# The last pair of expert half tiles: placed by one-hot products and added by GpSimd, or scattered with the rest

## The reference, cut to what matters

```python
def _L1_ffn_ref(hidden_states, gate_w, gate_up_proj, down_proj):
    B, S, H, E, I, TOPK = (1, 256, 512, 16, 256, 2)
    ...
    p = jax.nn.sigmoid(logits)
    p = p / jnp.sum(p, axis=-1, keepdims=True)
    w, idx = jax.lax.top_k(p, TOPK)
    w = w / jnp.sum(w, axis=-1, keepdims=True)
    combine = jnp.sum(jax.nn.one_hot(idx, e, dtype=w.dtype) * w[..., None], axis=1)
    gu = jnp.einsum('th,ehf->etf', x, gate_up_proj)
    gate, up = jnp.split(gu, 2, axis=-1)
    inter = jax.nn.silu(gate) * up
    y = jnp.einsum('eti,eih->eth', inter, down_proj)
    out = jnp.einsum('eth,te->th', y, combine.astype(y.dtype))
```

## Time and profile before

| what | value |
|---|---|
| median of 3 runs | 2191.06 us (2190.95 to 2192.75) |
| the profiled execution | 2190.56 us |
| its span, first to last instruction | 2188.8 us |
| PE busy | 2079.7 us, 95% of the span |
| DVE, ACT, POOL busy | 1566.5, 1253.0, 573.9 us |
| data moved | 202.02 MB |

### The profile page before, as it was taken

One profiled execution on the slowest core, in us unless ns is written; L12 is line 12 of the kernel. 1 busy time (PEld: TensorE's weight loads), 2 busy tenths in 40 slices (PEclk: granted clock), 3 DMA queues, 4 the chain that ended last, 5 costly groups with the idle time before them and its releaser, 6 DMA issues. The chain is left out here.

```text
span 2188.8 us, 36050 instructions
## 1 busy us (share of the span) xinstructions
PE 2079.7 (95%) x11652; PEld 1792.7 (82%) x11652; DVE 1566.5 (72%) x3714; ACT 1253.0 (57%) x3253; POOL 573.9 (26%) x1480
## 2 busy tenths in 40 slices
PE   7999999999999999999899999999999999599992
PEld 6888988988888778887788888888888887388882
DVE  6777687677779884434677777777777777777775
ACT  5554455445455533324776766677676666567771
POOL 2001011001001002223333434433343433145541
PEclk9999999999999999999999999999999999799996
DMA  7232122122220220002111211111111111278886
GB/s 255 78 116 74 66 87 90 59 90 68 85 78 34 75 75 1 1 0 78 49 59 49 72 53 57 48 57 48 57 64 71 48 40 39 87 272 291 292 272 257
DMA packets 78500, 202.02 MB, mean 92 GB/s; under 512 B 8688, under 2 KB 38408, under 8 KB 66208
## 3 DMA queue, kind: packets, MB, share of 16 engines
q1 hardware_dynamic: 68672, 179.37, 23.5%
q0 software_dynamic: 7520, 16.80, 2.3%
q10 hardware_dynamic: 2176, 4.19, 0.5%
HBM read 179.09 MB, written 29.10 MB: 95 GB/s over the span
## 5 line engine op out<-in xcount | busy, mean ns | idle before, releaser
L1255 DVE TENSOR_TENSOR l_pT_lo<-bank,l_pT_hi 128x512 fp32r<-128x512 f32 x256 | 175.3, 685 | 69.7 <-ACT l_pT_hi L1081 69.7
L742 PE MATMUL bank<-l_wkv_hi,l_ctxT 128*128 128x512 f32 (+1 forms) x768 | 222.3, 361 | 2.7 <-DVE l_v_lo L1255 1.6
L1075 ACT ACTIVATE l_probs<-l_scored,l_nbias 128x256 f32<-128x256 f32 x256 | 128.5, 505 | 165.7 <-DVE l_nbias L1328 165.7
L742 PE MATMUL bank<-l_wo_hi,l_oT_hi 128*128 128x512 f32 x512 | 209.1, 408 | 0.7 <-DVE l_oT_lo L1255 0.7
L742 PE MATMUL bank<-xnT_hi,l_wq_hi 128*128 128x512 f32 x512 | 209.0, 408 | 0.8 <-DVEq L1561 0.7
L742 PE MATMUL bank<-l_wo_hi,l_oT_lo 128*128 128x512 f32 x512 | 200.5, 392 | 0.0
L742 PE MATMUL bank<-xnT_hi,l_wq_lo 128*128 128x512 f32 x512 | 200.2, 391 | 0.0
L742 PE MATMUL bank<-l_wo_lo,l_oT_hi 128*128 128x512 f32 x512 | 199.9, 390 | 0.0
L742 PE MATMUL bank<-xnT_lo,l_wq_hi 128*128 128x512 f32 x512 | 199.8, 390 | 0.0
L1081 ACT CAST l_pT_hi<-bank 128x512 fp32r<-128x512 f32 x256 | 150.8, 589 | 67.5 <-PE bank L841 67.4
L1343 DVE TENSOR_SCALAR l_probs<-l_probs,l_rden 128x256 f32<-128x256 f32 x512 | 181.3, 396 | 9.0
(11 more groups left out here) (307 smaller groups left out, 5754.0 us busy)
## 6 DMA issues: line engine op xcount, KB each, us to landing
l_ctxT<-ctx_split SPq DMA_DIRECT2D x63, 1024.0 KB, 4.8
moe_raw_gu<-in_L_ffn_gate_up_proj SPq DMA_DIRECT2D x31, 1024.0 KB, 6.7
moe_raw_dn<-in_L_ffn_down_proj SPq DMA_DIRECT2D x31, 512.0 KB, 5.5
l_raw_a<-in_L_xattn_Wq SPq DMA_DIRECT2D x16, 512.0 KB, 5.9
l_raw_a<-in_L_xattn_Wo SPq DMA_DIRECT2D x16, 512.0 KB, 5.8
x_sb<-in_x SPq DMA_DIRECT2D x4, 1024.0 KB, 8.8
l_v_next<-l_kn SPq DMA_DIRECT2D x16, 256.0 KB, 2.0
l_v_lo<-l_v_next SPq DMA_DIRECT2D x16, 256.0 KB, 2.7
```

The lines of the kernel that those rows point to most:

```text
L742: mm = nc.tensor.matmul(out, a[x], b[y], start=(i == 0), stop=(i == n - 1))
L1075: ins = nc.scalar.activation(probs[u % 2][:, t, :], src, ACT.Exp, bias=nbias[:, i:i + 1], scale=scale, accum_out=rsum[:, i:i + 1])
L1255: nc.vector.tensor_tensor(pair[1], src, pair[0].bitcast(F32), ALU.subtract).then_inc(done, 1)
```

## The change

The 45 halves 0 to 44 are scattered as before. The last pair, halves 45 and 46, is not. `SENT = HALVES - 2` counts those that are sent.

- Where no scatter writes, `y_rows` must hold zeros: the FFN stage fills all 8.39 MB with zeros in four transfers from one tile.
- The routing marks which tokens stand in the last pair. GpSimd counts the numbers 0 to 2047 in one instruction and casts them in four. DVE works out each token's weight for the last pair (`weigh_last`, round 3) and two one-hot matrices of 128 rows by 2048 tokens, one for each half (`mark_tokens`, rounds 6 and 9).
- Behind the last down products, the results of halves 45 and 46 are split into high and low parts. For each of the 16 token tiles TensorE multiplies them by the one-hot matrices (4 products of 512 columns), ScalarE scales the sum by the weight, and GpSimd adds it to `x_sb`. DVE's two additions for a tile wait for that.
- The loads of `y_rows` wait for 15 scatters in each of three semaphores instead of for 16, 16 and 15. The buffers `w_gu[1]` are taken before `w_gu[0]`.
- In round 46, `down(44)` and its copy come ahead of `gate_up_products(46)` and of `gate(46)`.
- For lack of semaphores those of the FFN stage are cleared and used again; the clearing stands ahead of the two gain loads of the second attention.

```diff
@@ attention_stage, sync
             if rms:
+                for s in k.past_sems:
+                    sp.sem_clear(s)
@@ ffn_stage
+        zeros, y_cleared = sb("zeros", [P, D]), k.layer_sem("y_cleared")
+        y_fill = k.y_rows.rearrange("(i n p) d -> p i n d", p=P, i=CLEARS)
...
             start.load_dsc(sp, dsc)
+            sp.wait_ge(y_cleared, 1)
+            across = [P, y_fill.shape[2], D]
+            for i in range(CLEARS):
+                sp.dma_start(y_fill[:, i], zeros[:, :].rearrange("p (o d) -> p o d", o=1).broadcast_to(across)).then_inc(y_cleared, 16)
             sp.wait_ge(up_made, NF * (NG - 1) + 8)
...
+            pool.wait_ge(cleared, 1)
+            nc.gpsimd.memset(zeros[:, :], 0.0).then_inc(y_cleared, 1)
@@ moe_stage
+    SENT = HALVES - 2
-        both_rows = [raw_gu[0][:, :], raw_gu[1][:, :]] + [w[i][:, :].bitcast(F32) for w in w_gu for i in range(2)]
+        both_rows = [raw_gu[0][:, :], raw_gu[1][:, :]] + [w_gu[b][i][:, :].bitcast(F32) for b in (1, 0) for i in range(2)]
+        scaled_rows = [raw_dn[b][:, D * i:D * (i + 1)] for b in (1, 0) for i in range(2)]
+        b_last = [banks[7], *banks[0:4]]
@@ sync
-            for s, b in enumerate(y_out):
-                sp.wait_ge(b, 16 * (PAIRS if s < 2 else SINGLES))
+            for b in y_out:
+                sp.wait_ge(b, 16 * (SENT // STEPS))
+            for b in range(2):
+                sp.wait_ge(wg_split[b], 2 * loads_before[b])
             for n in range(NT // 2):
                 due(sp, summed, 2 * (n - 5))
+                if n in (2, 4):
+                    sp.wait_ge(gu_made, HALVES if n == 4 else SENT)
@@ gpsimd
             for r in rows[1:]:
                 gp.memset(r[:, :], 0.0).then_inc(consts_made, 1)
+            gp.iota(token_no_i, pattern=[[GT, KD], [1, GT]], base=0, channel_multiplier=0).then_inc(tokens_counted, 1)
+            pool.wait_ge(tokens_counted, 1)
+            for c in range(KD):
+                ins = gp.tensor_copy(token_no[:, c, :], token_no_i[:, c, :])
+            ins.then_inc(tokens_counted, 1)
...
+            pool.wait_ge(y_cleared, 16 * CLEARS + 1)
-            for n in range(HALVES + 2 * STEPS):
+            for n in range(SENT + 2 * STEPS):
...
+            for t in range(NT):
+                pool.wait_ge(last_scaled, t + 1)
+                row = k.x_sb[:, t, :]
+                gp.tensor_tensor(row, row, scaled_rows[t % 4], ALU.add).then_inc(last_added, 1)
@@ tensor
                     if n + 1 < HALVES:
                         turn_x(n + 1)
+                    else:
+                        down(n - 2)
                     gate_up_products(n)
...
-                if n >= 2:
+                if 2 <= n < HALVES - 1:
                     down(n - 2)
...
+            def place_last(t):
+                due(pe, last_scaled, t - len(b_last) + 1)
+                if t == 0:
+                    pe.wait_ge(tokens_marked, 2)
+                for h in range(2):
+                    if t == 0:
+                        pe.wait_ge(last_split, h + 1)
+                    for part in range(2):
+                        mm = nc.tensor.matmul(b_last[t % len(b_last)][:, :], to_token[h][:, t // TG, P * (t % TG):P * (t % TG + 1)],
+                                              last_y[h][part], start=(h == 0 and part == 0), stop=(h == 1 and part == 1))
+                mm.then_inc(last_placed, 1)
+            for t in range(NT):
+                place_last(t)
@@ scalar
+                if n == HALVES - 1:
+                    copy_y(n - 2)
                 gate(n)
...
-            copy_y(HALVES - 2)
-            copy_y(HALVES - 1)
+            for h in range(2):
+                act.wait_ge(y_made, SENT + h + 1)
+                nc.scalar.copy(last_y[h][0], b_y[(SENT + h) % 2][:, :]).then_inc(last_hi, 1)
+            def scale_last(t):
+                act.wait_ge(last_placed, t + 1)
+                if t < 4:
+                    act.wait_ge(wd_split[1 - t // 2], loads_before[1 - t // 2])
+                due(act, last_added, t - 3)
+                nc.scalar.activation(scaled_rows[t % 4], b_last[t % len(b_last)][:, :], ACT.Copy, scale=last_weight[:, t:t + 1]).then_inc(last_scaled, 1)
             ov = out.rearrange("b (t p) d -> p (b t) d", p=P)
+            for t in range(4):
+                scale_last(t)
             for n in range(NT // 2):
+                for t in range(2 * n + 4, min(2 * n + 6, NT)):
+                    scale_last(t)
                 act.wait_ge(summed, 2 * (n + 1))
@@ vector
+            def weigh_last():
+                chain(v.tensor_scalar(last_parts[:, :, :], half[:, :, :], 2.0 * PAIRS, None, ALU.is_lt))
+                chain(v.scalar_tensor_tensor(last_parts[:, :, :], half[:, :, :], 2.0 * (PAIRS - 1), last_parts[:, :, :], ALU.is_ge, ALU.mult))
+                for c, weight in enumerate((m1, m2)):
+                    chain(v.tensor_tensor(last_parts[:, c, :], last_parts[:, c, :], weight[:, :], ALU.mult), c == 1)
+                chain(v.tensor_tensor(last_weight[:, :], last_parts[:, 0, :], last_parts[:, 1, :], ALU.add), False)
+                chain(v.tensor_copy(last_token[:, :], token_of[:, 2 * (PAIRS - 1):2 * PAIRS]))
+                dve.wait_ge(tokens_counted, 2)
+            def mark_tokens(h):
+                v.tensor_scalar(to_token[h], token_no, last_token[:, h:h + 1], None, ALU.is_equal).then_inc(tokens_marked, 1)
...
+                if n == STEPS:
+                    weigh_last()
+                if n in (2 * STEPS, 3 * STEPS):
+                    mark_tokens(n // STEPS - 2)
                 fuse_up(n)
...
+            for h in range(2):
+                dve.wait_ge(last_hi, h + 1)
+                v.tensor_tensor(last_y[h][1], b_y[(SENT + h) % 2][:, :], last_y[h][0].bitcast(F32), ALU.subtract).then_inc(last_split, 1)
             for t in range(NT):
...
+                dve.wait_ge(last_added, t + 1)
                 for c, weight in enumerate((m1, m2)):
```

More of the change, by code:

```diff
@@ L40 @@
 LATE = 2 * TG
+CLEARS = 4
 FIRST = (2, 3)
@@ L1726, in sem @@
         def sem(n):
-            return k.sem(f"ffn_{n}")
+            s = k.sem(f"ffn_{n}")
+            k.past_sems.append(s)
+            return s
         w = start.w
@@ L2070, in moe_stage @@
     ACT_TILES = [t for t in range(LATE, NT) if t not in DVE_TILES]
-    y_rows = nc.dram_tensor("moe_y_rows", (2 * T, D), F32, kind="Internal").ap()
+    y_rows, y_cleared = k.y_rows, k.layer_sem("y_cleared")
     gu_v = gate_up.rearrange("e (p k) f -> e p (k f)", p=P)
@@ L2080, in sem, with freed_sem @@
             return k.sem(f"moe_{n}")
+        def freed_sem():
+            return k.past_sems.pop()
         def pair(n, shape):
@@ L2120, in moe_stage @@
         m1, m2, ms, key = (sb(n, [P, NT]) for n in ("m1", "m2", "ms", "key"))
+        last_weight, last_parts, last_token = sb("last_weight", [P, NT]), sb("last_parts", [P, 2, NT]), sb("last_token", [P, 2])
+        token_no_i = at_place("token_no_i", k.xnT_hi_at, [P, KD, T], I32)[:, :, GT:2 * GT]
+        token_no = at_place("token_no", k.xnT_lo_at, [P, KD, T], F32)[:, :, GT:2 * GT]
+        to_token = [k.xnT_hi[:, :, GT * g:GT * (g + 1)] for g in (1, 2)]
+        last_y = [[k.xnT_hi[:, 2 * h + part, 3 * GT:4 * GT] for part in range(2)] for h in range(2)]
         WIDTH = E + P + 2 * PAIRS + NT + 2
@@ L2149, in moe_stage @@
         summed, stored = sem("summed"), sem("stored")
+        tokens_counted, tokens_marked, last_hi, last_split, last_placed, last_scaled, last_added = (freed_sem() for _ in range(7))
         b_x, b_gu, b_f, b_y = banks[0:2], banks[2:4], banks[4], banks[5:7]
@@ L2712, in decoder_layers @@
         k.layer_sem = layer_sem
+        k.past_sems = []
         k.banks = [st.enter_context(nc.psum_tensor(f"bank{i}", [P, 512], F32)) for i in range(8)]
@@ L2720, in decoder_layers @@
         k.ctx_split = nc.dram_tensor("ctx_split", (NG, P, 2 * KC * GT), F32, kind="Internal").ap()
-        k.x_in, k.ctx_stored, k.ln0_chain = [k.sem(f"x_in{i}") for i in range(3)], k.sem("ctx_stored"), k.sem("ln0_chain")
+        k.x_in, k.ctx_stored, k.ln0_chain = [k.sem(f"x_in{i}") for i in range(3)], k.sem("ctx_stored"), k.layer_sem("ln0_chain")
         k.ln_stats = st.enter_context(nc.sbuf_tensor("ln_stats", [P, NT, 6], F32))
@@ L2738, in decoder_layers @@
         start = attention_start(k, None, "l1", *w1[:3], rms=True, at=nc.sbuf_base)
+        k.layer_sems["y_cleared"] = k.layer_sems.pop("ln0_chain")
+        k.y_rows = nc.dram_tensor("moe_y_rows", (2 * T, D), F32, kind="Internal").ap()
         ffn_stage(k, ffn, start)
```

## The result

After: 2200.01 us, the median of 6 runs (2197.29 to 2201.96), against 2191.01 in 6 runs of before (2188.12 to 2192.75). The ratio is 1.0042, 95% interval 1.0031 to 1.0053: 9.0 us slower, within 6.8 to 11.6. The profiled execution took 2197.29 us, its span 2195.5.

A forecast was written before the change was run, and what follows sets the result against it. At the end, full DMA transfers bound the sum, with DVE only 2.5 us behind. DVE's start -3.7, its stretch +12.3 and routing +1.5 make +10.1: 2201 us (likeliest case, chance 0.65, 2196 to 2207; overall range 2193.5 to 2207).

The forecast's parts named there:

- The first load 5.95 earlier: End of kernel: loads of `y_rows` wait for half 44, not 46, so the first goes out 5.95 us earlier.
- DVE's start, -3.7: Final sum: DVE starts at 2155.6, when GpSimd's first addition is done, 3.7 us earlier than before.
- Strict turns, +12.3: Final sum: GpSimd and DVE alternate at the SBUF inputs, so DVE's stretch grows from 26.34 to 38.65 us.
- Nothing else in the sum: Final sum: TensorE's 64 products and ScalarE's 16 scalings run ahead of DVE and cost nothing.
- The routing, +1.5: Start of routing: GpSimd's count and casts delay DVE's normalisations, 1.5 us, range 0.5 to 2.6.
- the dear case: Start of routing: casts go in between DVE's normalisations, making the first low part 2.1 us late instead of 0.6.
- At nothing: marks and fill: Expert loop and FFN stage: small DVE marking instructions and the 21 us zero fill are covered and cost nothing.
- Rival 1: Final sum: GpSimd and DVE overlap without turns, transfers stay the limit, 2186.7 us; chance 0.10.
- The limit of 0.47: Final sum: Rival 1 decides where GpSimd holds the inputs under p = 0.47 us per addition, against 1.15 expected.
- Rival 2: Final sum: turns fall partly in holes DVE leaves anyway, saving half the lock's 14.8; +2.7, 2193.8 us; chance 0.10.
- Rival 3: Whole instructions are paid in the final sum, or the marks stall TensorE: +14.6, 2205.7 us; chance 0.15.
- The lower bound: Final sum: with a GpSimd addition of 0.95 us, DVE's stretch would be 35.5 us, 3.2 less than forecast.

The follow-up runs named there:

- nothing placed: Changed kernel without TensorE's placing products, ScalarE's scalings, GpSimd's additions and DVE's wait for them (last pair's rows missing): 2185.41 us, ratio 0.9976 against before.
- only written: Changed kernel with GpSimd filling a spare tile with zeros instead of adding, all waits and handoffs kept: 2186.71 us, ratio 0.998 against before.
- no wait: Changed kernel with GpSimd's 16 additions going into a spare tile and DVE not waiting for them: 2197.63 us, ratio 1.0031 against before.
- additions in before: Kernel before the change, plus 16 unneeded GpSimd additions into a spare tile during the sum, nobody waiting: 2204.04 us, ratio 1.0062 against before.
- half the width: Changed kernel with GpSimd adding only 256 of the 512 columns: 2191.43 us, ratio 1.0003 against before.
- the later counting: Changed kernel with GpSimd counting and casting token numbers only after DVE's four normalisations: 2199.08 us, ratio 1.0034 against before.
- the last two versions: Changed kernel, later count, TensorE putting `x_sb` into the bank, no GpSimd additions: 2189.7 us (0.9992 against before); with three identity products made early, 2187.77 us (0.9986).

## Why the prediction was right

The forecast of 2201 and its likeliest case hold, in sign and cause. That it lies 1.0 from the median is partly luck: its sum was +10.1, two of its terms were too large by 1.0 and 0.9, and the stage's own rows give 8.2. The medians differ by 9.0; the other 0.8 is inside the interval and put down to no stage. Its terms one by one:

- **The first load 5.95 earlier.** Measured from the first turn of gathered rows it is 228.19 against 234.98, so 6.8 earlier. The scatters of halves 43 and 44 were issued only 1.44 apart, as the copies were, and SyncE's issue came 2.23 behind the last scatter's, not 2.78. Nothing hung on it: DVE waited for the addition.
- **DVE's start, -3.7.** It was -3.82. In the chain cast 0.60, low part 0.70, products 0.75, scaling 0.70 and addition 1.30 stand one behind the other.
- **Strict turns, +12.3.** It was +11.32. The step is right: with the lock taken away in two ways (nothing placed, only written) the stretch is 26.4 and 24.4, and with the lock alone (no wait, additions in before) it is 38.6 and 38.4. The size was 1.0 too large, since a pair hides 0.36 and not 0.29: 15 x 1.67 + 17 x 0.73 = 37.5, measured 37.66.
- **Nothing else in the sum.** Right: with TensorE's and ScalarE's work kept and GpSimd only writing, the stretch is 24.4, shorter than before.
- **The routing, +1.5.** This term was mis-sized: it was about 0.6. What the prediction took for the dear case did happen, casts and normalisations one by one. But TensorE's turn was issued 8.72 behind the first statistics against 7.40 before, so 1.32 late and not 2.1, and between it and the loop about half of this was absorbed. Where, I didn't separate. The count was read a little dear too: rows 7 give 0.8 ns a number, not 0.9 to 1.0, and it took 1.84.
- **At nothing: marks and fill.** Right. The two marks take 1.28 each (1.22 had been the one row), and TensorE's turns of halves 0 and 46 lie 218.0 apart, against 218.3 before. The fill is issued from 800.74 on, under products. With nothing placed, both are in the kernel and it is faster than before.
- **Rival 1**, the transfers stay the limit, would have given 2186.7; the two kernels without the lock took 2185.41 and 2186.71. So its price was right, and its condition is what fails. By the prediction's own formula, the 1.67 of a pair less 0.60 puts p at 1.07. The limit of 0.47 was also misread: it is where the change would cost nothing; for the rival's own price DVE has to end 5.95 earlier, at 2179.7, and that takes p below 0.18. At half the width the stretch of 29.5 gives p = 0.54, and that kernel is no faster than before.
- **Rival 2**, turns in holes, was not seen: DVE left no hole. **Rival 3**, whole instructions paid, would be a pair of 2.03; the row shows 1.67.
- **The lower bound** of the stretch was worked wrong: an addition of 0.95 less the hidden 0.14 gives 33.6, not 35.5. Nothing hung on it, since an addition takes 1.29.

The Trainium skill's page "SBUF — State Buffer", section "Who interferes with whom", calls the shared pair of ports an exclusive lock and says, of DVE's two-port modes, that whoever issues first has it for the whole instruction. On who blocks whom the traces agree. Carried over to this case as the prediction did, the whole instruction is too much, and the measurement decides: 0.36 of each pair is hidden, 5.4 us over 15 pairs.

The change in one line: it takes 6.8 us from the loads, loses 3.0 of them to the placing ahead of the first sum, and pays 11.3 for the lock behind it and 0.6 for the counting.

## What to carry to other kernels

Before work goes to an idle engine, ask whether it can run beside the engine that is next to the limit. GpSimd reading SBUF beside DVE instructions with two SBUF inputs is not parallel: 1.29 beside 0.75 is 1.67 for a pair. Find a pair of such rows anywhere in the trace and sum them over the stretch; a few odd rows of other stages priced DVE's stretch here to 1.0 in 11.3 us. And where a stage has 2.5 us of slack, give it a new operand in an existing instruction (here an addend from a PSUM bank), not a new instruction.

## What the runs showed that I had not expected

- Two queues full of work alternate one for one. Neither engine gets two turns in a row in 16 rounds, and the rows of both give 1.67 to 1.69 a pair.
- GpSimd's pauses in the changed kernel don't pay: they only spread the turns over a longer time, and the number of DVE instructions that wait stays 15.
- The instructions that wait in the routing are others. A `memset` of GpSimd delayed no scalar-tensor-tensor (0.745 to 0.753). But a 4-element tensor-scalar of DVE took 1.04 beside two of them, in the traces of before and after alike, where the same line takes 0.21 to 0.27 a little earlier. And the normalisations, with one SBUF tensor as input, took 1.75 beside the count and 0.82 or 0.83 each beside the casts, against 0.54 alone. That GpSimd is the cause is shown for the normalisations, by the later counting; for the 1.04 it is inferred.
- A float32 product of 128x512 by the identity shows as two instructions and 0.86 us at a granted clock of 1.00, where the four placing products of `fp32r` parts took 0.92 together. It cost the first of the last two versions much of its gain.
